# SyncE's order at the end of an image: the edge row moved ahead of the four corner transfers of the ring

## Chip, cores and metric

The program runs on one core of one Trainium2 chip. The metric is the device time of one launch in microseconds (us); less is better. The times are those of whole launches, and one execution was also profiled.

## The reference, cut to what matters

```python
def step(u, _):
    ux, uy, uxx, uxy, uyy = _derivs(u)                  # 3x3 Sobel stencils, and stencils of stencils
    g2 = ux * ux + uy * uy
    ...                                                 # curvatures K and H from the five fields
    diff = jnp.clip(alpha * K + beta * H, -1.0, 1.0)
    u = u + DT * diff
    u = jnp.pad(u[:, :, 1:-1, 1:-1], ((0, 0), (0, 0), (1, 1), (1, 1)), mode='edge')
    return (u, None)
u, _ = jax.lax.scan(step, x, None, length=10)
x = 0.7 * u + 0.3 * x                                   # the "blend"
out = conv(relu(conv(x, w1) + b1), w2) + b2 + x         # second stage
```

There are 8 x 16 = 128 images of 512 x 512 in float32. After each of the ten steps the outermost pixels of an image are overwritten with their inner neighbours: first the edge columns, then the edge rows (which read corners that the columns have set).

## The kernel before, in words

**Tiling.** An image is cut into patches so that 128 partitions hold 2048 pixels each; partition p holds every 16th row and every 8th column. An image has two halves ("chunks") of 1024 pixels a partition. Four images are in work at once, so one step is eight chunks, c = 0 to 7, and each image is carried through ten steps. There are 32 rounds of four images. Neighbouring pixels lie in other partitions, so a step needs matmuls over partitions (the stencils, L654) and a "ring" of neighbours shifted by a row or a column, which is copied inside SBUF by DMA.

**The ring.** `exchange(image, j, part)` (L288) issues four DMAs from `tame_split` to `tame_halo`. Part 0 holds left, right, top and bottom (520, 520, 260 and 260 KB); part 1 holds the four corners (65 KB each, from and to 4 partitions). The stencils of both chunks of an image wait for all eight.

**Periods.** All engines walk through periods k = 0 to 7 of a step. In period k TensorE works on chunk k, VectorE ends chunks k-1 and k-2, and SyncE sets the edges of chunk k-2: `edge_columns` (two small DMAs, L297, after `updated`), and `edge_rows` (one DMA, L305 for even and L307 for odd chunks, after both columns have landed). In every even period SyncE also issues the ring of the image that comes two periods later. GpSimd issues one DMA a period, which adds K to U (`add_k`, L379).

**End of an image.** In the tenth step (body "closing", and the first two periods of the next one, "opening") each chunk is also blended into the staging tile: VectorE's `blend` (`tame_stage<-tame_U,tame_stage`, listed under L532) in the period after its edges. It waits for the chunk's edge row (`rows_done`) and for ScalarE's `scale` of the staged input (L468). It stands on VectorE ahead of `curvature_k`, which TensorE's `uxx` waits for. After a blend, SyncE loads the next image's half (`load_half`, L277, 512 KB), after the second half of an image it stores the staging tile (`store`, L311, 1 MB), and in periods 5 and 7 of closing it loads a staging tile (`load_stage`, L283, 1 MB) once the store before has landed. All of these are in SyncE's one order, and each of its instructions waits for the one ahead.

In the first-stage body a chunk "ends" when its tenth step is done: chunks 0 to 5 in periods 2 to 7 of closing, chunks 6 and 7 in periods 0 and 1 of opening. Only in the even ones of these periods is there a part 1 of a ring to issue beside an edge row: chunks 0, 2, 4 and 6.

Of the kernel before, what the change touches and what calls it, by code (L numbers as in the profile page):

```python
# [54 lines left out]
def place(c):  # L55

    return c // 2 + (1 - c % 2) * (PC // 2)
# [50 lines left out]
def curvature_flow(nc, keep, semaphores, x, alpha, beta, stencils, mixed, tame):  # L108
# [21 lines left out]
    with ExitStack() as ctx:  # L130
# [80 lines left out]
        def half(c):  # L211
            return U[:, c % CHUNKS // 2, c % 2 * HALF:(c % 2 + 1) * HALF]

        def half_rows(c):
            return half(c).rearrange("p (y x) -> p y x", x=PX)
# [12 lines left out]
        def done(t, c):  # L228
            return t + 2 * (c + 1)

        def split_done(t, c):
            return t + 2 * (c + 1) + BODY

        def exists(kind, c):
            return not (kind == "first" and c < 0) and not (kind == "tail" and c >= 0)

        def ends(kind, c):
            return (kind in ("closing", "last") and c >= 0) or (kind in ("opening", "tail") and c < 0)

        def goes_on(kind, c):  # L240

            return not (kind == "last" and c >= 0) and not (kind == "tail" and c < 0)
# [7 lines left out]
        def walk(eng, period):  # L250
            def body(t, kind, r=None):
                for k in range(CHUNKS):
                    period(t, k, kind, r)

            body(0, "first")
            with eng.Fori(BODY, (STEPS - 1) * BODY, BODY) as t:
                body(t, "middle")
            with eng.Fori(0, ROUNDS - 1) as r:
                body(r * (STEPS * BODY) + (STEPS - 1) * BODY, "closing", r)
                body(r * (STEPS * BODY) + STEPS * BODY, "opening", r)  # L260
                with eng.Fori((STEPS + 1) * BODY, (2 * STEPS - 1) * BODY, BODY) as t:
                    body(r * (STEPS * BODY) + t, "middle")
            body((ROUNDS * STEPS - 1) * BODY, "last", ROUNDS - 1)
            body(ROUNDS * STEPS * BODY, "tail", ROUNDS - 1)
# [3 lines left out]
        @block.sync  # L268
        def _(sp):
            sp.dma_start(a_raw, alpha.partition_broadcast(P)).then_inc(params_in, 16)  # L270
            sp.dma_start(b_raw, beta.partition_broadcast(P)).then_inc(params_in, 16)
            sp.dma_start(stage[0][:, 0:MATRICES * P].rearrange("p (n m) -> p n m", m=P),
                         stencils[:, 0:MATRICES, :]).then_inc(stencils_in, 16)
            sp.dma_start(unit[:, :, :], stencils[:, MATRICES:, :]).then_inc(unit_in, 16)

            def load_half(r, k):
                sp.dma_start(half(k), x[bass.ds(r * SLOTS + k // 2, 1), :, k % 2 * HALF:(k % 2 + 1) * HALF].rearrange(  # L277
                    "o p c -> (o p) c")).then_inc(x_in[k], 16)

            def load_stage(r, i):  # L280
                sp.wait_ge(stored[i % 2], r * 32 + (i // 2 * 16 + 16))
                sp.sem_inc(stage_free, 1)
                sp.dma_start(stage[i % 2][:, :], x[bass.ds(r * SLOTS + i, 1), :, :].rearrange(  # L283
                    "o p c -> (o p) c")).then_inc(stage_in[i % 2], 16)

            def exchange(i, j, part):
                for first, step, n, shift, to, apart in RING[part * 4:part * 4 + 4]:
                    sp.dma_start(halo[j][to:to + (n - 1) * apart + 1:apart, :, :].bitcast(F32),  # L288
                                 split[i][first:first + (n - 1) * step + 1:step, :,
                                          BEFORE + shift:BEFORE + shift + RUN].bitcast(F32)).then_inc(halo_in[i], 16)  # L290

            def edge_columns(t, c):
                u = half_rows(c)
                sp.wait_ge(updated, done(t, c))
                signal = columns_done[c % CHUNKS]
                for edge, inner, px in ((0, 1, 0), (PC - 1, PC - 2, PX - 1)):
                    sp.dma_start(u[place(edge):P:PC, :, px:px + 1], u[place(inner):P:PC, :, px:px + 1],  # L297
                                 allow_slow_non_contiguous=True).then_inc(signal, 16)

            def edge_rows(t, c):  # L300
                u = half_rows(c)
                sp.wait_ge(columns_done[c % CHUNKS], t * 2 + (32 if c >= 0 else 0))
                signal = rows_done[c % CHUNKS]
                if c % 2 == 0:
                    sp.dma_start(u[0:PC, 0:1, :], u[PC:2 * PC, 0:1, :]).then_inc(signal, 16)  # L305
                else:
                    sp.dma_start(u[P - PC:P, ROWS - 1:ROWS, :], u[P - 2 * PC:P - PC, ROWS - 1:ROWS, :]).then_inc(signal, 16)  # L307

            def store(r, i):
                image = mixed[bass.ds(r // (C // SLOTS), 1), :, bass.ds(r % (C // SLOTS) * SLOTS + i, 1), :, :]  # L310
                sp.dma_start(image.rearrange("b r o g c -> (b r o) g c"), stage[i % 2][:, :]).then_inc(stored[i % 2], 16)  # L311

            def period(t, k, kind, r):
                filling = k % 2 == 0 and kind != "tail" and not (kind == "last" and k == CHUNKS - 2)
                image, j = (k + 2) % CHUNKS // 2, (k + 2) % 4 // 2
                if filling:
                    sp.wait_ge(lo_ready, split_done(t, k - 5))
                    sp.sem_inc(split_whole, 1)
                    if not (kind == "first" and k == 0):
                        sp.wait_ge(product[LAST_FIELD], done(t, k - 1))  # L320
                    exchange(image, j, 0)
                c = k - 3
                ending = exists(kind, c) and ends(kind, c)
                if ending:
                    sp.wait_ge(blended, r * CHUNKS + (c % CHUNKS + 1))
                    sp.sem_inc(stage_done, 1)
                    if goes_on(kind, c):
                        load_half(r + 1, c % CHUNKS)
                c = k - 2
                if exists(kind, c):  # L330
                    edge_columns(t, c)
                if filling:
                    exchange(image, j, 1)
                if exists(kind, c):
                    edge_rows(t, c)
                c = k - 3
                if ending and c % 2:
                    store(r, c % CHUNKS // 2)
                if k in (5, 7) and kind in ("closing", "last"):
                    load_stage(r, k // 2)  # L340
                if k in (6, 7) and kind in ("first", "opening"):
                    load_stage(0 if kind == "first" else r + 1, k - 6)

            for k in range(CHUNKS):
                load_half(0, k)
            for j in range(2):
                sp.sem_inc(stored[j], 16)
            sp.wait_ge(stencils_rounded, 1)
            sp.wait_ge(ring_zeroed, 1)
            sp.wait_ge(lo_ready, 4)  # L350
            exchange(0, 0, 0)
            exchange(0, 0, 1)
            walk(sp, period)
            for j in range(2):
                sp.wait_ge(stored[j], ROUNDS * 32 + 16)
# [675 lines left out]
```

## Time and profile before

| what | us |
|---|---|
| median of 3 runs | 36501.38 |
| lowest and highest of them | 36483.21, 36510.54 |
| profiled execution, its time | 36543.25 |
| its span | 36541.3 |
| TensorE busy in the span | 33388.0 |
| VectorE busy | 31917.9 |
| ScalarE busy | 32731.5 |

The profiled execution took 41.9 us more than the median of the runs, and its span is 2.0 us under its own time. A steady round of 8 chunks runs from about 1.3 ms to 32.8 ms of the span; the second stage fills the rest and has none of the code in question.

### The profile page before, as it was taken

The page shows a single profiled execution, that of the slowest core. Times are in us where ns is not written, and L with a number is a line of the kernel's source. Part 1 is how long each engine was busy: PE and PEld are TensorE (multiplying, and loading weights), DVE is VectorE, ACT ScalarE, POOL GpSimd, SP SyncE. Part 2 cuts the span into 40 slices and gives each one's busy share as a digit, 9 for nine tenths or more (in the row PEclk, how much of TensorE's full clock was granted, in tenths as well). Part 3 has the DMA queues.
Part 4 walks back from the last instruction along what each step waited for, and adds up shares of the span by engine and source line. Part 5 has one row for each costly group of instructions (what it writes and reads, how often), then busy time and mean ns, then how long its engine had stood idle before and what let it go on. Part 6 is the DMA issues. An engine that isn't in the chain of part 4 may idle for free. (4 is left out here: it accounts for less than half of the span.)

```text
span 36541.3 us, 454649 instructions
## 1 busy us (share of the span) xinstructions
PE 33388.0 (91%) x126400; PEld 23480.4 (64%) x126400; DVE 31917.9 (87%) x30550; ACT 32731.5 (90%) x33722; POOL 21233.1 (58%) x10245
## 2 busy tenths in 40 slices
PE   5999999999999999999999999999999999989999
PEld 3666666666666666666666666666666666666666
DVE  8999999999999999999999999999999999991111
ACT  5999999999999999999999999999999999993333
POOL 3666666666666666666666666666666666660000
PEclk9999999999999999999999999999999999999999
DMA  6555555555555555555555555555555555553333
GB/s 222 129 129 130 128 124 122 130 128 129 129 129 129 129 129 124 124 129 129 129 129 129 129 129 129 125 121 129 129 130 129 129 129 129 129 115 86 87 87 87
DMA packets 3056143, 4603.99 MB, mean 126 GB/s; under 512 B 2307140, under 2 KB 2307268, under 8 KB 2733380
## 3 DMA queue, kind: packets, MB, share of 16 engines
q1 hardware_dynamic: 2686276, 3247.70, 35.7%
q0 software_dynamic: 368640, 1342.34, 19.7%
q8 instruction: 475, 7.78, 0.1%
q14 instruction: 752, 6.16, 0.1%
HBM read 582.33 MB, written 268.44 MB: 23 GB/s over the span
## 5 line engine op out<-in xcount | busy, mean ns | idle before, releaser
L654 PE MATMUL tame_slot<-tame_split,tame_M 128*128 128x512 f32 x51200 | 14727.2, 410 | 2992.1 <-ACT tame_ux L415 1768.1
L654 PEld LDWEIGHTS tame_slot<-tame_split,tame_M 128*128 128x128 f32 x51200 | 9360.1, 190 | 7792.7 <-ACT tame_ux L415 3880.2
L654 PE MATMUL tame_slot<-tame_halo,tame_M 128*128 128x512 f32 x51200 | 14283.6, 401 | 25.3 <-issue 25.0
L654 PEld LDWEIGHTS tame_slot<-tame_halo,tame_M 128*128 128x128 f32 x51200 | 9735.2, 190 | 2518.6 <-issue 31.4
L367 POOL TENSOR_TENSOR tame_ux<-tame_ux,tame_uy 128x1024 f32<-128x1024 f32 x2560 | 6146.6, 2401 | 2765.6 <-DVE tame_uy L532 2765.5
L379 POOL DMA_DIRECT2D tame_U<-tame_slope x2560 | 2241.6, 876 | 8448.8 <-DVE tame_slope L586 8181.0
L373 POOL TENSOR_TENSOR tame_ux<-tame_ux,tame_cross 128x1024 f32<-128x1024 f32 x2560 | 6939.1, 2711 | 0.0
L361 POOL TENSOR_TENSOR tame_split<-tame_U,tame_split 128x1024 fp32r<-128x1024 f32 x2560 | 6710.6, 2622 | 21.6 <-ACT tame_split L404 21.6
L442 ACT ACTIVATE tame_slope<-tame_slope 128x2048 f32<-128x2048 f32 x2560 | 4912.2, 1919 | 234.9
L664 PE MATMUL tame_slot<-tame_uxy,tame_unit 128*128 128x512 f32 x10240 | 4815.1, 593 | 6.3 <-DVE tame_slot L555 4.2
L532 DVE SCALAR_TENSOR_TENSOR tame_cross<-tame_cross,tame_slot 128x1024 f32<-128x1024 f32 x2560 | 3122.3, 1220 | 664.2 <-issue 613.3
L532 DVE SCALAR_TENSOR_TENSOR tame_U<-tame_slope,tame_par,tame_U 128x1024 f32<-128x1024 f32 x2560 | 3307.5, 1292 | 14.4 <-DMA tame_U<-tame_slope 14.0
L532 DVE SCALAR_TENSOR_TENSOR tame_slope<-tame_slot,tame_par,tame_slope 128x1024 f32<-128x1024 f32 x2560 | 3258.3, 1273 | 4.1 <-PE tame_slot L664 3.2
L555 DVE TENSOR_TENSOR tame_slot<-tame_uyy,tame_slot 128x1024 f32<-128x1024 f32 x2560 | 3128.5, 1222 | 0.0
L551 DVE TENSOR_TENSOR tame_cross<-tame_cross,tame_slot 128x1024 f32<-128x1024 f32 x2560 | 3092.5, 1208 | 40.1 <-PE tame_slot L654 39.8
L580 DVE TENSOR_TENSOR tame_slope<-tame_ux,tame_slot 128x1024 f32<-128x1024 f32 x2560 | 3108.3, 1214 | 3.9 <-issue 3.9
L532 DVE SCALAR_TENSOR_TENSOR tame_uy<-tame_uy,tame_slot 128x1024 f32<-128x1024 f32 x2560 | 3107.9, 1214 | 0.0
L532 DVE SCALAR_TENSOR_TENSOR tame_slope<-tame_ux,tame_uy 128x1024 f32<-128x1024 f32 x2560 | 3105.2, 1213 | 2.8 <-ACT tame_uy L421 2.7
L532 DVE SCALAR_TENSOR_TENSOR tame_ux<-tame_ux,tame_slot 128x1024 f32<-128x1024 f32 x2560 | 3094.1, 1209 | 8.6 <-ACT tame_uyy L427 8.2
L437 ACT ACTIVATE tame_slope<-tame_slope 128x1024 f32<-128x1024 f32 x2560 | 2755.6, 1076 | 280.9 <-DVE tame_slope L532 274.3
L870 DVE SCALAR_TENSOR_TENSOR res<-po,vec,xin 96x512 f32<-96x512 f32 x672 | 501.6, 746 | 2839.3 <-PE po L891 2839.3
L823 ACT ACTIVATE hid<-ph,vec 128x512 f32<-128x512 f32 x2064 | 754.6, 437 | 2421.8 <-PE ph L891 2421.8
(75 smaller groups left out, 40812.1 us busy)
## 6 DMA issues: line engine op xcount, KB each, us to landing
tame_halo<-tame_split SPq DMA_DIRECT2D x2560, 520.0 KB
tame_U<-tame_slope POOLq DMA_DIRECT2D x2560, 512.0 KB, 5.2
tame_halo<-tame_split SPq DMA_DIRECT2D x2560, 260.0 KB
tame_halo<-tame_split SPq DMA_DIRECT2D x5120, 65.0 KB
tame_U<-in_x SPq DMA_DIRECT2D x256, 512.0 KB, 6.0
tame_stage<-in_x SPq DMA_DIRECT2D x128, 1024.0 KB, 6.1
mixed<-tame_stage SPq DMA_DIRECT2D x128, 1024.0 KB, 6.5
out<-res SPq DMA_DIRECT2D x672, 192.0 KB
```

What stands on the lines that cost most here:

```text
L361: nc.gpsimd.tensor_tensor(split_rows(c, 1), half_rows(c), split_rows(c, 0).bitcast(F32), ALU.subtract).then_inc(lo_ready, 2)
L367: nc.gpsimd.tensor_tensor(ux2[c % 2][:, :], ux2[c % 2][:, :], uy2[c % 2][:, :], ALU.add).then_inc(sum_h, 2)
L373: nc.gpsimd.tensor_tensor(ux2[c % 2][:, :], ux2[c % 2][:, :], cross[c % 2][:, :], ALU.add).then_inc(num_h_ready, 2)
L379: pool.dma_start(half(c), slope[c % 2][:, 1, :], accum_op=ALU.add).then_inc(k_added[c % 2], 16)
L437: nc.scalar.activation(slope[c % 2][:, 1, :], slope[c % 2][:, 0, :], ACT.Square).then_inc(slope2_ready, 2)
L442: nc.scalar.activation(both, both, ACT.Ln, bias=EPS).then_inc(logs_ready, 2)
L532: return nc.vector.scalar_tensor_tensor(out=out, in0=a, scalar=s, in1=b, op0=op0, op1=op1)
L551: nc.vector.tensor_tensor(cross[c % 2][:, :], cross[c % 2][:, :], ps["uy"][:, :], ALU.mult).then_inc(cross_ready, 2)
L555: nc.vector.tensor_tensor(ps["uxx"][:, :], uyy[:, :], ps["uxx"][:, :], ALU.mult).then_inc(prod_k, 2)
L580: nc.vector.tensor_tensor(slope[c % 2][:, 0, :], ux2[c % 2][:, :], inverse[:, :], ALU.mult).then_inc(h_ready, 2)
L654: last = nc.tensor.matmul(ps[name][:, b * BANK:(b + 1) * BANK], M[0:lanes, matrix, :], rows(c, part)[:, b * y:(b + 1) * y, :], start=(n < ...
L664: last = nc.tensor.matmul(ps["uxx"][:, b * BANK:(b + 1) * BANK], unit[:, 0, :], uxy2[:, b * BANK:(b + 1) * BANK], start=False, stop=True, ...
```

## The change

For a chunk whose image ends, `edge_rows` is called directly behind `edge_columns`, and part 1 of the ring behind it. For every other chunk the order stays as it was. Nothing is added or removed: one DMA and its wait are moved ahead of four DMAs.

```diff
                 c = k - 2
+                late = exists(kind, c) and not ends(kind, c)
                 if exists(kind, c):
                     edge_columns(t, c)
+                    if not late:
+                        edge_rows(t, c)
                 if filling:
                     exchange(image, j, 1)
-                if exists(kind, c):
+                if late:
                     edge_rows(t, c)
                 c = k - 3
                 if ending and c % 2:
```

SyncE in period 6 of closing: `tame_U<-tame_U 16x16x1` are the edge columns of chunk 4, `8x64` its edge row, `4x2x2080 x4` the four corners, and `mixed<-tame_stage` the store of the image before:

```order
 L297 DMA tame_U<-tame_U 16x16x1 [waits updated]
 L297 DMA tame_U<-tame_U 16x16x1
+L305 DMA tame_U<-tame_U 8x64 [waits columns_done4]
 L288 DMA tame_halo<-tame_split 4x2x2080 x4
-L305 DMA tame_U<-tame_U 8x64 [waits columns_done4]
 L311 ISA
 L311 DMA mixed<-tame_stage 16x8x2048
```

The edge row and its wait for the columns now stand ahead of the corners, and the corners stand directly ahead of the store.

SyncE in period 0 of opening, the same for chunk 6:

```order
 L297 DMA tame_U<-tame_U 16x16x1 [waits updated]
 L297 DMA tame_U<-tame_U 16x16x1
+L302 REGISTER_ALU
+L305 DMA tame_U<-tame_U 8x64 [waits columns_done6]
 L288 DMA tame_halo<-tame_split 4x2x2080 x4
-L302 REGISTER_ALU
-L305 DMA tame_U<-tame_U 8x64 [waits columns_done6]
 L311 ISA
 L311 DMA mixed<-tame_stage 16x8x2048
```

Here too the four corners move behind the wait. Chunks 0 and 2 are moved alike in periods 2 and 4 of closing.

What stands on SyncE between these two places (period 7 of closing, and the start of opening), in the kernel before; it is the same after the change:

```order
L277 DMA tame_U<-in_x 128x1024
L297 DMA tame_U<-tame_U 16x16x1 [waits updated]
L297 DMA tame_U<-tame_U 16x16x1
L307 DMA tame_U<-tame_U 8x64 [waits columns_done5]
L283 ISA [waits stored1]
L283 DMA tame_stage<-in_x 128x2048
L317 REGISTER_ALU
L288 DMA tame_halo<-tame_split 32x2x2080 [waits lo_ready,uxx_product]
```

Nothing moves here, but all of it waits for what was issued ahead of it: chunk 5's row waits for chunk 5's columns, the staging load stands behind that row, and part 0 of the next ring behind the load.

## Rows read from the trace of the kernel before

**Rows 1.** The page's span and its busy times of the engines.
```profile
span 36541.3 us, 454649 instructions
...
PE 33388.0 (91%) x126400; PEld 23480.4 (64%) x126400; DVE 31917.9 (87%) x30550; ACT 32731.5 (90%) x33722; POOL 21233.1 (58%) x10245
```

**Rows 2.** Waits of the whole span (us, times, longest), then who waited for L305.
```profile
DVE tame_stage L532 <- DMA tame_U<-tame_U: 282.0, 63, 6.1
...
  DVE tame_stage L532: 277.8, 62
```

**Rows 3.** Timeline of SyncE's queue, first round: start, us until issued, line, DMA.
```profile
1360.40 3.75 SPq L288 DMA_DIRECT2D tame_halo<-tame_split  x4
...
1389.12 5.16 SPq L297 DMA_DIRECT2D tame_U<-tame_U  x2
1394.33 2.58 SPq L288 DMA_DIRECT2D tame_halo<-tame_split  x4
1399.04 0.70 SPq L305 DMA_DIRECT2D tame_U<-tame_U  x1
1400.03 0.65 SPq L311 DMA_DIRECT2D mixed<-tame_stage  x1
1402.37 0.35 SPq L277 DMA_DIRECT2D tame_U<-in_x  x1
1404.52 1.26 SPq L297 DMA_DIRECT2D tame_U<-tame_U  x2
1410.68 0.71 SPq L307 DMA_DIRECT2D tame_U<-tame_U  x1
1411.68 0.34 SPq L283 DMA_DIRECT2D tame_stage<-in_x  x1
1414.97 3.94 SPq L288 DMA_DIRECT2D tame_halo<-tame_split  x4
1420.86 4.32 SPq L297 DMA_DIRECT2D tame_U<-tame_U  x2
...
1429.63 0.71 SPq L305 DMA_DIRECT2D tame_U<-tame_U  x1
```

**Rows 4.** Timeline of VectorE, the blends of chunks 3 to 6 in that round.
```profile
1383.14 1.32 DVE L532 SCALAR_TENSOR_TENSOR tame_stage<-tame_U,tame_stage 128x1024 f32<-128x1024 f32 x1 [0.69 <-ACT tame_stage L468]
...
1400.88 1.23 DVE L532 SCALAR_TENSOR_TENSOR tame_stage<-tame_U,tame_stage 128x1024 f32<-128x1024 f32 x1 [4.57 <-DMA tame_U<-tame_U]
...
1416.28 1.23 DVE L532 SCALAR_TENSOR_TENSOR tame_stage<-tame_U,tame_stage 128x1024 f32<-128x1024 f32 x1 [1.50 <-ACT tame_stage L468]
...
1432.14 1.23 DVE L532 SCALAR_TENSOR_TENSOR tame_stage<-tame_U,tame_stage 128x1024 f32<-128x1024 f32 x1 [2.77 <-DMA tame_U<-tame_U]
```

**Rows 5.** Timeline, the last of the 62 pairs of edge row and waiting blend.
```profile
31838.29 0.71 SPq L305 DMA_DIRECT2D tame_U<-tame_U  x1
...
31841.15 1.23 DVE L532 SCALAR_TENSOR_TENSOR tame_stage<-tame_U,tame_stage 128x1024 f32<-128x1024 f32 x1 [5.31 <-DMA tame_U<-tame_U]
```

**Rows 6.** Issue to landing: columns of chunk 4, then the staging load at 1411.68.
```profile
DMA to landing us min/median/max: 6.4/7.1/7.8
...
DMA to landing us min/median/max: 4.9/4.9/4.9
```

**Rows 7.** Stretches of that round: us, busy times, granted clock, DMA share, GB/s.
```profile
1398.00:1400.50 2.50, 1.86 (x8) 1.37 (x8) 0.00 (x0) 2.50 (x3) 0.00 (x0) 1.00 0.10 37
1401.00:1410.50 9.50, 5.58 (x16) 3.95 (x16) 9.50 (x9) 4.47 (x4) 3.91 (x3) 0.70 0.93 221
1410.50:1412.50 2.00, 2.00 (x8) 1.57 (x7) 1.89 (x3) 1.03 (x2) 2.00 (x2) 0.73 0.01 1
1412.50:1416.00 3.50, 3.29 (x11) 1.70 (x11) 1.54 (x2) 3.50 (x4) 2.37 (x1) 1.00 0.81 300
1416.00:1426.00 10.00, 8.62 (x36) 6.29 (x35) 9.72 (x9) 9.60 (x10) 4.03 (x3) 1.00 0.98 236
1426.00:1429.50 3.50, 3.15 (x11) 1.60 (x10) 3.26 (x4) 3.50 (x5) 3.50 (x2) 1.00 0.65 129
```

**Rows 8.** Timeline of TensorE: the first stencil of the next round's chunk 0.
```profile
1407.63 2.04 PE L654 MATMUL tame_slot<-tame_split,tame_M 128*128 128x512 f32 x4 [1.58 <-DVE tame_ux L532]
```

## Prediction

> **What bounds the kernel now.** I read the page first. TensorE is busy for 91% of the span, ScalarE for 90% and VectorE for 87% [rows 1], so in the steady steps all three are near their limit and SyncE only has to be in time. The change touches SyncE alone, and only at the end of images, so I went from the page to the waits. There the blend stands with 282.0 us in 63 waits for an edge DMA, and the look from the other side says that 62 of these are for L305, the edge row of an even chunk, with 277.8 us [rows 2]. That is two in each of 31 rounds (the last round has no ring to fill), 4.5 us each.
>
> Which two, the timelines tell. Blends of undisturbed chunks wait 0.69 us for ScalarE; chunk 4 waits 4.57 us and chunk 6 waits 2.77 us for the row DMA, and chunk 5 between them 1.50 us for ScalarE [rows 4]. From chunk 3's blend to chunk 4's it is 17.74 us. The longer wait is passed on in full, since VectorE has work without a gap in the rest of that period, and TensorE and ScalarE hang on it. Chunks 0 and 2, which the change moves too, have no such wait. So what the change is worth hangs on the two places with chunk 4 and chunk 6, 31 times each, and one us there is 31 us in the total.
>
> **Why the row is late there.** In SyncE's queue [rows 3] the columns of chunk 4 need 5.16 us to be issued, the corners go out from 1394.33 to 1396.91, and then SyncE stands still until 1399.04, when it issues the row. The columns took 6.4 to 7.8 us from issue to landing [rows 6]: the second, issued about 1392.6, landed about 1399.0. So SyncE waited 2.13 us for the columns with the corners already out. The corners in front cost the row no issue time: after the change its wait ends at the same moment, if the columns land at the same moment. At chunk 6 it is alike: the row goes out at 1429.63, well behind the corners.
>
> **What moves, part by part.**
>
> Issue of the row: nothing gained at chunks 4 and 6, by the above. At chunks 0 and 2 it goes out earlier (for chunk 2 it stood behind 3.75 us of corners [rows 3]), where the blend does not wait for it; worth nothing.
>
> Landing of the row: in the first round the blend of chunk 4 started 1.84 us behind the issue of its row (1400.88 - 1399.04), that of chunk 6 2.51 us behind (1432.14 - 1429.63) [rows 3, 4], the last pair 2.86 us [rows 5]. Over the 62 pairs, of which these are the first and the last, the mean is 2.38 us, and the shortest is about 1.8 us. I read the excess as the tail of the corners, which are still moving on some engines when the row comes. With the corners behind the row I take 1.84 us for all: 0.54 x 62 = **33 us gained**. Bounds: nothing, if the excess is other traffic; and if the corners slow the columns too, up to 1.3 us a place, 81 us, since the time from the columns' issue to the blend is 11.8 us at chunk 4 (1389.12 to 1400.88) and 11.3 us at chunk 6, and with the row's excess gone and the columns in time it could be about 10.3.
>
> The Trainium skill (DMA: Bandwidth & Descriptors, Queues, rings and completion order) says that a copy is split over up to 16 rings, always the lowest-numbered, and that each ring is consumed in its order. By that rule a row of 8 partitions shares its rings with corners of 4 partitions and waits behind them, while columns that were issued ahead of the corners don't. The spread from 1.84 to 2.86 us agrees with it. By the rule the gain would be the 33 us and not the 81.
>
> Issue of the corners: they no longer go out at 1394.33 but behind the row, at 1399.04 + 0.71 = 1399.8. Four took 2.58 us here and 3.75 us in a calmer place [rows 3]; I take 3.2, so SyncE is free at 1403.0 where it was free at 1399.8. **Everything behind on SyncE is 3.2 us late** (2.6 to 3.8): the store of 1 MB, issued at 1403.3 for 1400.03; load_half about 1404.2 for 1402.37; the columns of chunk 5 hardly, since they wait for `updated` until 1404.52.
>
> The Trainium skill (the same page, Anatomy of one DMA) has a rule that speaks against this order: DMA engines never wait for a semaphore, the issuing sequencer does, so what stands behind a wait isn't even queued. Here the row's wait falls in a stretch where the DMA engines have a share of 0.10 [rows 7], and the corners would have filled it.
>
> What this does to the DMA engines: after 1401 they were busy without a pause, share 0.93, until 1410.5 with the store, the load, the columns of chunk 5 and GpSimd's add [rows 7], and the columns of chunk 5 landed at the end of it, since L307 went out at 1410.68 [rows 3]. The block starts 3.2 us later, so it ends about 1413.9 and chunk 5's row goes out there. With 1.84 us it is there at 1415.7; the blend of chunk 5 starts at 1416.28, held by ScalarE [rows 4]. That cover of 0.6 us just hides it: cost 0, and up to 1 us (31 us in all) where it is thinner.
>
> But behind chunk 5's row on SyncE stands the staging load (1 MB, 1411.68, 4.9 us to landing [rows 3, 6]). It fell into an idle stretch (share 0.01 until 1412.5), and its data was through at 1416, just where part 0 of the next ring, issued at 1414.97, began to move [rows 3, 7]. Issued at 1414.9 instead, its data comes in front of the ring's: the ring, the load of chunk 5's successor and then chunk 6's columns are pushed back. From 1416 to 1426 the engines have a share of 0.98 and then 0.65 [rows 7], so a push at the front comes out nearly whole at chunk 6's columns, and the blend of chunk 6 waits for just those. At full size this is 3.2 us; the tail at 0.65 and rounds in which chunk 5's columns come earlier than here give a part back. I take 2.5 us: 2.5 x 31 = **78 us lost** (bounds 0, if the engines take the load in their gaps, and 3.8 x 31 = 118).
>
> Behind chunk 6 the same shift of 3.2 us meets chunk 7, but no staging load stands there and the next ring starts after a pause; I take 0 there, at most 1 us x 31.
>
> The corners themselves: issued until 1403.0, their stencils start at 1407.63 [rows 8], where TensorE waits for VectorE. Landed within 4.6 us of issue they cost nothing; in that stretch they have only the store beside them. I take 0.
>
> **Sum.** -33 + 78 = +45 us. Against the profiled execution of 36543.3 that is 36588; its 41.9 us above the median of the runs is no part of this, so for the median I predict 36501.4 + 45 = **36546 us**.
>
> **The rivals.**
>
> 1. Gain alone. The late staging load slips in beside the ring's parts, since single stretches of the ring may be slow for reasons other than busy engines. For it: 33 us of gain need nothing further. Against it: the share of 0.98. Time: 36501 - 33 = 36468 (to 36440).
> 2. Columns and row both come earlier, as the corners are out of the engines' way: 1.3 us x 62 = 81 us with no push, 36420. For it: chunk 4's columns need 4.7 us after the end of their issue. Against: they are ahead of the corners in the queue.
> 3. TensorE waits for the corners at the start of the next round's chunks 0 and 2, or the push is whole and chunks 5 and 7 wait as well. Place: the first stencil at 1407.63. It decides if the corners need more than 4.6 us after their issue; every us beyond is 62 us. With 1 us there and the sum above 36608; with 118 + 31 + 31 - 33 instead, 36648. For it: corners have been slow to land beside other traffic. Against: the engines are nearly empty when they now go out.
> 4. No effect at all: the row's excess is other traffic and the push is hidden, 36501.
>
> A longer or shorter wait also meets TensorE's clock: in the stretch behind chunk 4's wait the granted clock averages 0.70, part of it at the lower level (1.2 of 2.4 GHz) after TensorE stood still [rows 7], and the matmuls at 1407.63 are slow [rows 8]. Such a drop follows both waits already in most rounds, so I count no more than 10 us for it, either way.
>
> **How the numbers follow.** My sum with its neighbours, +10 to +90 us: 0.43. Rival 1: 0.25. Rival 4: 0.07. Rival 2: 0.10. Rival 3: 0.15. About 0.2% of the time, 73 us, is what a measurement of this kernel can tell from no change. Over +73 lie rival 3 and a quarter of my own case: 0.26. Under -73 lies most of rival 2: 0.10. The rest, 0.64, is within. The range takes in rival 1 whole, half of rival 2 and the near part of rival 3: 36430 to 36610. The likeliest case has 36511 to 36591 for itself.
>
> **What would show it.** In the changed trace the row of chunk 4 should go out in 1.84 us before its blend, with the corners behind it; chunk 4's wait should be about 0.5 us shorter than its mean of before. L307 of chunk 5 should stand about 13 us behind chunk 4's blend where it stood 9.8, the staging load behind it, and the wait of chunk 6's blend should be about 2 us longer. If chunk 6's wait is no longer than before, the push is wrong and rival 1 holds; if TensorE has a new wait for a `tame_halo` DMA, rival 3 does. The wait of the blends for DMAs, 282.0 us before, should come to about 330 us. I am wrong if the columns themselves land earlier, or if the four corners go out in far less than 2.6 us.

## The result and the profile after

The changed kernel takes 36584.1 us (median of 19 runs, 36558.8 to 36604.8) where the kernel before takes 36502.7 us (19 runs, 36472.0 to 36523.8). The ratio is 1.0021, with a 95% interval of 1.0015 to 1.0028: slower by 81 us, small but clear. Forecast were +45 us (36546 us) and a range from 36430 to 36610 us.

The blend's waits, in the view of waits of the changed kernel (us, times, longest), then the blend's waits for L305 and for L307 by themselves:

```profile
DVE tame_stage L535 <- DMA tame_U<-tame_U: 419.5, 120, 7.8
...
DVE tame_stage L535 <- ACT tame_stage L471: 106.2, 134, 1.7
...
  DVE tame_stage L535: 286.5, 62
...
  DVE tame_stage L535: 133.0, 58
```

Against [rows 2] the waits for an even chunk's row (L305) are as many as before and a little longer, 286.5 us for 277.8. What is new are 58 waits, 133.0 us, for L307, the row of an odd chunk, a line that the change doesn't touch. The blend's waits for ScalarE went down by 60.4 us (166.6 us in 191 times before), as they are now covered by the longer ones. Sum: 137.5 - 60.4 = 77 us more, close to the launch's 81 us. (The two profiled executions themselves are 61.5 us apart, see below the table.)

SyncE's queue in the first round of the changed kernel, timeline, as in [rows 3]:

```profile
1386.07 5.61 SPq L297 DMA_DIRECT2D tame_U<-tame_U  x2
1396.23 0.72 SPq L305 DMA_DIRECT2D tame_U<-tame_U  x1
1397.01 2.35 SPq L288 DMA_DIRECT2D tame_halo<-tame_split  x4
1399.64 0.66 SPq L311 DMA_DIRECT2D mixed<-tame_stage  x1
1400.66 0.35 SPq L277 DMA_DIRECT2D tame_U<-in_x  x1
1401.73 3.76 SPq L297 DMA_DIRECT2D tame_U<-tame_U  x2
1411.81 0.74 SPq L307 DMA_DIRECT2D tame_U<-tame_U  x1
1412.84 0.34 SPq L283 DMA_DIRECT2D tame_stage<-in_x  x1
1413.37 4.68 SPq L288 DMA_DIRECT2D tame_halo<-tame_split  x4
```

And VectorE's blends of chunks 4 to 7, as in [rows 4]:

```profile
1398.09 1.23 DVE L535 SCALAR_TENSOR_TENSOR tame_stage<-tame_U,tame_stage 128x1024 f32<-128x1024 f32 x1 [4.86 <-DMA tame_U<-tame_U]
1413.71 1.23 DVE L535 SCALAR_TENSOR_TENSOR tame_stage<-tame_U,tame_stage 128x1024 f32<-128x1024 f32 x1 [2.54 <-DMA tame_U<-tame_U]
1433.15 1.23 DVE L535 SCALAR_TENSOR_TENSOR tame_stage<-tame_U,tame_stage 128x1024 f32<-128x1024 f32 x1 [6.35 <-DMA tame_U<-tame_U]
1448.60 1.22 DVE L535 SCALAR_TENSOR_TENSOR tame_stage<-tame_U,tame_stage 128x1024 f32<-128x1024 f32 x1 [2.37 <-DMA tame_U<-tame_U]
```

What to see: the row of chunk 4 is followed by its blend after 1.86 us, with the corners behind it, as the change means it. But the store stands 1.55 us behind that blend, where it stood 0.85 us ahead of it [rows 3, 4], and the row of chunk 5 goes out 13.7 us behind the blend of chunk 4, where it was 9.8. Chunk 5's blend, held by ScalarE before, now waits 2.54 us for that row, and chunk 7's waits 2.37 us for its own.

The DMA engines in that round (us, busy times, granted clock, DMA share, GB/s), as in [rows 7]:

```profile
1395.00:1397.50 2.50, 1.86 (x8) 1.43 (x8) 0.00 (x0) 2.50 (x4) 0.00 (x0) 1.00 0.02 3
1398.00:1411.00 13.00, 9.95 (x28) 6.85 (x28) 12.81 (x12) 7.48 (x8) 7.21 (x4) 0.74 0.77 182
1411.00:1413.00 2.00, 1.64 (x7) 1.01 (x6) 0.17 (x1) 2.00 (x3) 1.09 (x1) 1.00 0.04 8
...
1416.50:1428.00 11.50, 9.44 (x36) 6.33 (x35) 10.19 (x10) 10.14 (x10) 8.31 (x4) 1.00 0.97 236
```

While SyncE waits for the columns the engines have nothing (0.02), then a block of 13 us at 0.77 where there was one of 9.5 us at 0.93: the same store, load, columns and add, started later, with the corners in it too.

From blend to blend, the mean over 31 rounds, worked out from the starts of the blends in both traces:

| from chunk to chunk | before, us | after, us | x 31, us |
|---|---|---|---|
| 3 to 4 | 17.87 | 17.49 | -12 |
| 4 to 5 | 14.57 | 15.76 | +37 |
| 5 to 6 | 17.36 | 18.24 | +27 |
| 6 to 7 | 14.56 | 15.43 | +27 |

The sum is +79 us. The stretches up to chunk 3 are the same to 0.02 us. The rest of a round, from chunk 7's blend through the other nine steps to the next chunk 0, took 907.91 us before and 907.42 after; it lies between 907.1 and 909.0 us in all thirteen traces, so these 0.5 us are not put down to the change. They are why the two profiled executions differ by only 61.5 us. A single stretch is not exact either: experiment 1 leaves the order at chunks 4 to 7 as it was and has 14.28 and 17.68 us from chunk 4 to 5 and from 5 to 6, for 14.57 and 17.36. So a row of the table can be off by some 10 us; the sum of those two is the same to 0.03 us.

GpSimd's add beside chunk 5's columns, before and then in the changed kernel, timeline of the first round:

```profile
1405.81 0.87 POOL L379 DMA_DIRECT2D tame_U<-tame_slope  x1 [8.55 <-DVE tame_slope L586]
```

```profile
1403.01 0.88 POOL L382 DMA_DIRECT2D tame_U<-tame_slope  x1 [8.85 <-DVE tame_slope L589]
```

Before, both columns were issued by 1405.78 [rows 3], just ahead of the add. In the changed kernel their issue takes 3.76 us, until 1405.49, and the second is still being issued when the add is out (1403.89). Before, the second column landed ahead of the add in all 31 rounds at chunk 5 and in 27 of 31 at chunk 7; after the change in none. Then both land together, 13.4 to 13.7 us behind the blend before, instead of 9.1 and 7.9 us for the column.

### The profile page after: what moved, and what is told of

The parts are those of the page before. It is cut to its first block and busy times, and to the rows that moved or that the text cites. A ratio compares the mean times of both kernels' runs of the same rounds, so it can differ in the third digit from the quotient of the medians.

```text
span 36602.9 us, 454649 instructions
## 1 busy us (share of the span) xinstructions
PE 33401.0 (91%) x126400; PEld 23460.5 (64%) x126400; DVE 31879.6 (87%) x30550; ACT 32759.2 (89%) x33722; POOL 21255.2 (58%) x10245
```

## The experiments

All were timed beside the kernel before on the same chip, so each ratio has its own "before" (36475 to 36503 us). The changed kernel stands at 1.0021 throughout. Mean waits by chunk, here and in the expectations, are over all 32 rounds; the last round waits 0.7, 0, 0 and 4.3 us at chunks 4 to 7 in nearly every run (in experiment 2, 7.4 at chunk 7). Times from blend to blend and from row to blend are means over the other 31.

**1. Only the calm places.** The change at chunks 0 and 2, not at 4 and 6 (the edit is to the changed kernel):

```diff
-                late = exists(kind, c) and not ends(kind, c)
+                late = exists(kind, c) and not (ends(kind, c) and 0 <= c < 4)
```

> The row goes ahead of the corners only at chunks 0 and 2 of an ending image; chunks 4 and 6 keep the order of before. Theory: all of the change's cost and gain lies at chunks 4 to 7, where blends wait for transfers, so this is the kernel before, 36503 us within 15 us. Rival (the two calm places cost or give something too, by the later store and load behind them): at least a quarter of the change's +81 us, or a gain of more than 20 us.

Measured: 1.0001 (0.9992 to 1.0010), 36483.1 us. Chunks 0 and 2 are worth nothing that can be told, and the effect comes from the two places where blends wait.

**2. Only the late store.** The kernel before, rows and corners in their old order, the two stores behind the next blend:

```diff
                     sp.sem_inc(stage_done, 1)
+                    if c % CHUNKS in (4, 6):
+                        store(r, c % CHUNKS // 2 - 1)
...
-                if ending and c % 2:
+                if ending and c % CHUNKS in (1, 7):
                     store(r, c % CHUNKS // 2)
```

> The kernel before, rows and corners where they were; only the stores that the change makes late (images of chunks 3 and 5) go out behind the next blend, at about 1.3 us behind the blends of chunks 4 and 6, where the changed kernel has them at 1.5 us and the kernel before at 1.4 us ahead. Theory (the later store and load ahead of the columns of chunks 5 and 7 make the loss): L307 of chunks 5 and 7 moves from 9.1 and 7.9 us to 12.5 to 14 us behind the blend before it, both blends get a wait for their row of 2.0 to 2.4 us, and the launch is 60 to 120 us over the kernel before. Rival (the corners' own data, now in that block, or SyncE's time for them is needed): L307 moves by less than 2 us and the launch by less than 40 us.

Measured: 1.0032 (1.0020 to 1.0044), 36605.7 us. SyncE's queue and the blends of its first round, timeline:

```profile
1394.97 0.66 SPq L311 DMA_DIRECT2D mixed<-tame_stage  x1
1395.82 0.43 SPq L277 DMA_DIRECT2D tame_U<-in_x  x1
1397.04 3.73 SPq L297 DMA_DIRECT2D tame_U<-tame_U  x2
1407.03 0.71 SPq L307 DMA_DIRECT2D tame_U<-tame_U  x1
```

```profile
1393.40 1.22 DVE L534 SCALAR_TENSOR_TENSOR tame_stage<-tame_U,tame_stage 128x1024 f32<-128x1024 f32 x1 [4.48 <-DMA tame_U<-tame_U]
1408.92 1.23 DVE L534 SCALAR_TENSOR_TENSOR tame_stage<-tame_U,tame_stage 128x1024 f32<-128x1024 f32 x1 [1.59 <-DMA tame_U<-tame_U]
```

The store stands 1.57 us behind chunk 4's blend, and chunk 5's row 13.6 us behind it: the changed kernel's numbers, with no corner and no row moved. Over the rounds chunks 5 and 7 wait 2.29 and 2.32 us (2.26 and 2.15 in the changed kernel, 1.05 and 1.23 before), and chunk 6's wait is 5.34 us. So the late store alone makes the loss: 1.0032, about 117 us. That it is more than the changed kernel's loss the times don't settle, as the intervals overlap. The stretches from blend to blend do: they sum to +112 us here and to +79 us there, and of the 33 us between, 14 lie in the stretch to chunk 4 and 17 in that to chunk 6, where the changed kernel's row lands faster.

**3. The store back in its place.** The changed kernel with the order row, store, corners (the store's lines further down are gone):

```diff
+                if ending and (k - 3) % 2:
+                    store(r, (k - 3) % CHUNKS // 2)
                 if filling:
                     exchange(image, j, 1)
```

> As the change, but the store of 1 MB goes out between row and corners, where the kernel before has it; only the corners are late. Theory: the loss comes from the store and the load that went out about 3 us later and reach into the columns of chunks 5 and 7. With the store back in time the block in front of those columns starts as before, the new waits of the blends of chunks 5 and 7 (2.26 and 2.15 us on average, 1.05 and 1.23 before) go back by at least half, and the launch takes 36500 to 36545 us. Rival (the corners themselves, now moved into that block, hold the columns up, wherever the store stands): the waits of chunks 5 and 7 stay at about 2.2 us and the time at 36570 to 36600. Corners could also come too late for TensorE's first stencil: then a wait for tame_halo appears and the time goes over 36600.

Measured: 1.0053 (1.0039 to 1.0067), 36671.8 us. Neither theory, but the warning at its end. The view of waits, and TensorE's first stencil of the next round's chunk 0 in the timeline:

```profile
PE tame_slot L656 <- DMA tame_halo<-tame_split: 737.0, 63, 415.0
PEld tame_slot L656 <- DMA tame_halo<-tame_split: 355.0, 66, 6.4
```

```profile
1410.73 1.65 PE L656 MATMUL tame_slot<-tame_split,tame_M 128*128 128x512 f32 x3 [5.01 <-DMA tame_halo<-tame_split]
```

One wait of 415 us at the start of the program is in every version; the 62 others, 5.2 us each, are new. Behind the store the four corners needed 5.78 us to be issued instead of 2.35, and came too late. On the store this run says less than it was made for, as TensorE's stall moves the blends of chunks 5 and 7 too; their rows go out 13.7 us behind the blend before, store early or not, as the columns now stand behind the slow corners. It shows how near the changed kernel is to that edge.

**4. The staging load behind the ring.** The changed kernel, with the load of period 7 behind part 0 of the next ring:

```diff
                     exchange(image, j, 0)
+                if k == 0 and kind in ("opening", "tail"):
+                    load_stage(r, 3)
...
-                if k in (5, 7) and kind in ("closing", "last"):
+                if k == 5 and kind in ("closing", "last"):
```

> As the change, but the staging load of period 7 goes out behind the first half of the next ring instead of ahead of it. Theory of the prediction (the late staging load pushes ring, load and columns of chunk 6): the wait of chunk 6's blend (4.77 us on average) falls by 1 to 2.5 us and the launch to 36510 to 36555 us. Rival (the wait of chunk 6 grew because later traffic in general is denser, and the same megabyte behind the ring is as much in the way of chunk 6's columns): that wait stays within 0.4 us and the time within 15 us of 36584.

Measured: 1.0034 (1.0022 to 1.0046), 36603.6 us; chunk 6's wait went up from 4.77 to 6.57 us. Both expectations missed. The megabyte is in front of the load and the columns in either place. From chunk 5's blend to chunk 6's it is 20.13 us for 18.24: the columns start to be issued 6.86 us behind chunk 5's blend instead of 5.19, and the row follows 11.4 us later for 11.2. So what the move cost is the later issue of the columns. My reading, not tried by itself, is that ahead of the ring a part of the megabyte still runs in an idle stretch and behind it none does. ScalarE also waits for this load now, 30.5 us in 23 waits.

**5. One store out of the way.** The changed kernel with the store of chunk 5's image behind chunk 7's row:

```diff
-                if ending and c % 2:
+                if ending and c % 2 and c % CHUNKS != 5:
                     store(r, c % CHUNKS // 2)
+                if ending and c % CHUNKS == 6:
+                    store(r, 2)
```

> The changed kernel, with one store (the image of chunk 5) taken out of the block ahead of chunk 7's columns and put behind chunk 7's row. Theory: the columns of chunk 7 land at least 3 us earlier, the wait of chunk 7's blend falls from 2.15 to about 1.2 us, the others stay, and the launch is 25 to 45 us under the changed kernel, at 1.0010 to 1.0015 of the kernel before. Rival (corners and load are enough to hold chunk 7's columns up): the wait stays over 1.8 us and the ratio at 1.002.

Measured: 1.0015 (1.0006 to 1.0024), 36532.1 us. Timeline of its queue and the blend of chunk 7:

```profile
1433.92 1.25 SPq L297 DMA_DIRECT2D tame_U<-tame_U  x2
1437.06 0.74 SPq L307 DMA_DIRECT2D tame_U<-tame_U  x1
```

```profile
1445.59 1.23 DVE L537 SCALAR_TENSOR_TENSOR tame_stage<-tame_U,tame_stage 128x1024 f32<-128x1024 f32 x1 [1.63 <-ACT tame_stage L473]
```

Over the rounds the columns of chunk 7 are through 1.9 us behind the end of their issue (6.2 in the changed kernel), and in all 31 ahead of GpSimd's add, the blend waits for ScalarE again, and its mean wait is 1.12 us. The corners and the load, still ahead of those columns, don't hold them up. The intervals of 1.0015 and 1.0021 overlap; the wait is what tells.

**6. Corners ahead of the columns.** The kernel before, and where an image ends: corners, columns, row.

```diff
+                early = filling and exists(kind, c) and ends(kind, c)
+                if early:
+                    exchange(image, j, 1)
                 if exists(kind, c):
                     edge_columns(t, c)
-                if filling:
+                if filling and not early:
                     exchange(image, j, 1)
```

> The kernel before with the other way to free the row: where an image ends, the corners go out ahead of the columns, and the row directly behind the columns. Theory (rows land in 1.8 us where no corner is behind the columns; the columns land only when ring, load and GpSimd's add are through, and the corners are a small part of that): row to blend falls from 2.4 to about 1.9 us, the store stays early, no new wait at chunks 5 and 7: 10 to 50 us under the kernel before. Rival (corners ahead of the columns hold these up by their full time of 1.5 to 3 us): chunk 4 and 6 wait longer and the launch is 30 to 150 us over it.

Measured: 1.0034 (1.0022 to 1.0046), 36611.1 us; the rival was right. Its queue, timeline:

```profile
1380.87 1.80 SPq L277 DMA_DIRECT2D tame_U<-in_x  x1
1382.71 6.91 SPq L288 DMA_DIRECT2D tame_halo<-tame_split  x4
1389.75 1.33 SPq L297 DMA_DIRECT2D tame_U<-tame_U  x2
1394.79 0.73 SPq L305 DMA_DIRECT2D tame_U<-tame_U  x1
```

Rows land fast (row to blend 1.88 us over the rounds), but behind ring and load SyncE needs 6.91 us to issue four corners. The columns of chunk 4 go out 13.0 us behind chunk 3's blend instead of 6.0, its row 18.0 instead of 15.5, and chunks 4 and 6 wait 6.5 and 6.3 us.

**7. The load behind the row.** The kernel before, and in all periods with a ring `load_half` behind the edge row instead of ahead of the columns:

```diff
-                    if goes_on(kind, c):
+                    if goes_on(kind, c) and not filling:
                         load_half(r + 1, c % CHUNKS)
...
                 c = k - 3
+                if ending and goes_on(kind, c) and filling:
+                    load_half(r + 1, c % CHUNKS)
```

> The kernel before with one other edit: in periods with a ring, load_half of an ending image goes out behind the edge row instead of ahead of the columns. Theory: what holds the rows of chunks 4 and 6 is the traffic in front of their columns (ring and 512 KB of load), not the corners; without the load in front the columns land 1.5 to 3 us earlier, and each of the two blend waits (4.6 and 4.1 us) falls by as much: 36503 less 60 to 180 us, 36320 to 36440. Rival (the columns are held by the ring and by GpSimd's add alone): no more than 30 us gained. Another (ScalarE's next high part waits for the load, which now lands 4 to 5 us later): a new wait of ScalarE for the load, and a time over 36503.

Measured: 0.9992 (0.9983 to 1.0001), 36443.5 us beside 36475.4: less than the theory's 60 us, and by time just short of clear. The two waits fell to 3.64 and 2.72 us, but chunk 2's row, calm before, became late (blend to blend 14.21 us for 13.72). The rows of chunks 4 and 6 go out about 2 us earlier (13.3 and 13.1 us behind the blend before, for 15.5 and 15.0), but with the corners still ahead of them they take longer to land: from row to blend 3.58 and 2.88 us instead of 2.39 and 2.36. ScalarE has a new wait:

```profile
ACT tame_split L406 <- DMA tame_U<-in_x: 100.4, 77, 2.8
```

**8. Both of these.** Corners ahead of the columns and the load behind the row (the edits of 6 and 7 together).

> Both: corners ahead of the columns, and in periods with a ring load_half behind the row. Theory: the columns have only ring, corners and add ahead, the row nothing; the waits of chunks 4 and 6 (3.64 and 2.72 us with the load behind the row alone) fall by another 1 us each, to about 2.6 and 1.8: 36475 less 60 to 120 us. Rival (ScalarE's high part waits for the late load in each of those periods, 1.3 us before, and takes the gain): no faster than with the load behind the row alone, ratio 0.9992.

Measured: 1.0018 (1.0009 to 1.0027), 36538.4 us; the rival was right on the side and it came out worse than it said. Rows land in 1.88 us, with the load right behind them, but the waits of chunks 4 and 6 are back at 4.58 and 4.78 us, since the columns go out 11.4 and 11.8 us behind the blend before instead of 3.9. ScalarE's wait for the load is 262.9 us.

**9. The change where it can't hurt.** Row first at chunk 6 alone, and the store of chunk 5's image behind chunk 7's row (an edit to the changed kernel; the store's lines are those of experiment 5):

```diff
-                late = exists(kind, c) and not ends(kind, c)
+                late = exists(kind, c) and not (ends(kind, c) and c % CHUNKS == 6)
```

> The change at chunk 6 alone (row ahead of the corners), chunks 0, 2 and 4 in the order of before, and the store of chunk 5's image behind chunk 7's row. Theory: this keeps the gain (row to blend of chunk 6 from 2.4 to 1.9 us) and leaves nothing late ahead of chunk 7's columns; chunk 5 has no late store and there is no late staging load. Blend waits of chunks 5 and 7 stay at 0.9 to 1.3 us, that of chunk 6 falls by about 0.5 us: 5 to 30 us under the kernel before, ratio 0.9992 to 1.0000. Rival (the row's landing behind the corners was never the limit, or the late corners cost TensorE): no gain, or over 1.0005.

Measured: 0.9995 (0.9986 to 1.0004), 36485.8 us. Row to blend at chunk 6 is 1.88 us, the waits of chunks 5 and 7 are 1.03 and 1.12 us, and chunk 6's is 3.53 us. As expected by size, and by size not to be told from no change.

**10. The edits of 9 and 7 together.**

> The same together with load_half behind the edge row in periods with a ring (0.9992 on its own). Theory: the two add up, since with the load gone from ahead of the columns the row of chunk 6 lands 2.8 us behind its issue, and without the corners 1.8: chunk 6's wait falls from 2.7 to about 1.7 us, ratio 0.9978 to 0.9990. Rival (the load is now behind the corners too and ScalarE waits for it longer than the row gains): ratio 0.9992 or more.

Measured: 0.9996 (0.9987 to 1.0005), 36484.2 us. Chunk 6's wait fell to 1.87 us, but the load now stands behind the corners too, ScalarE's wait for it grew to 192.2 us, and from chunk 6's blend to chunk 7's it is 15.83 us instead of 14.2. The rival was right.

**11. The load behind the row at chunks 4 and 6 only.** Only the two periods with a late row:

```diff
-                    if goes_on(kind, c):
+                    if goes_on(kind, c) and c % CHUNKS not in (3, 5):
                         load_half(r + 1, c % CHUNKS)
...
+                if ending and goes_on(kind, c) and c % CHUNKS in (3, 5):
+                    load_half(r + 1, c % CHUNKS)
```

> The kernel before with load_half behind the edge row only in the two periods where the blend waits for that row (chunks 4 and 6); chunks 2 and 0 keep their order. With it in all periods with a ring, the waits of chunks 4 and 6 fell to 3.64 and 2.72 us, but chunk 2's blend got a longer one (14.21 instead of 13.72 us from blend to blend). Theory: without that, 31 times 0.5 us more are saved: ratio 0.9984 to 0.9992, 20 to 60 us under the kernel before. Rival (the waits of chunks 4 and 6 fell because of what was moved at chunk 2, or ScalarE's waits for the late load take it all): 0.9995 or more.

Measured: 0.9976 (0.9967 to 0.9985), 36419.1 us beside 36503.1: faster than both kernels, by more than expected. Its waits, and its queue at chunk 4:

```profile
DVE tame_stage L534 <- DMA tame_U<-tame_U: 206.4, 64, 4.4
...
ACT tame_split L406 <- DMA tame_U<-in_x: 69.9, 55, 3.2
```

```profile
1380.40 4.47 SPq L297 DMA_DIRECT2D tame_U<-tame_U  x2
1384.92 3.91 SPq L288 DMA_DIRECT2D tame_halo<-tame_split  x4
1389.73 0.70 SPq L305 DMA_DIRECT2D tame_U<-tame_U  x1
1390.64 0.35 SPq L277 DMA_DIRECT2D tame_U<-in_x  x1
1391.26 0.65 SPq L311 DMA_DIRECT2D mixed<-tame_stage  x1
```

The row goes out 9.3 us behind the start of the columns' issue (9.9 before, [rows 3]), and the columns' issue starts earlier as the load's is gone from ahead of it. Blend to blend it is 16.88 and 15.91 us at chunks 4 and 6, 17.87 and 17.36 before: 2.4 us in a round, 76 us in all, and chunks 5 and 7 are 0.3 us shorter each. Against experiment 7 it is less clear than the ratios look: their intervals touch (0.9985 and 0.9983), and in the two traces the stretches up to chunk 7 differ by 0.46 us a round, 14 us in all, most of it at chunks 2 and 3.

## Why the prediction came out as it did

The side was right and the time is in the range. The terms that the prediction worked out were of the right kind, but most of the loss came from two that it had put at 0. With the measured gain and push alone the sum would be +11 us; that it came out near is in part luck, as the push was taken 35 us too large and the two zeros 64 us too small.

- **Where it counts.** The two places with chunks 4 and 6, 31 times each: right. Without them it is worth nothing that can be told (experiment 1).
- **The landing of the row, -33 us.** Right. Row to blend is 1.87 us over the 62 pairs instead of 2.38, so 0.51 x 62 = 32 us; none took more than 1.89 us, where it was up to 3.6 before. The columns themselves didn't come faster: issue to landing 6.4 to 7.6 us at chunk 4 in the first round for 6.4 to 7.8 [rows 6]. Rival 2 is out. Experiments 2 (order of before, 2.32 us) and 9 (row first at chunk 6, 1.88 us) agree.
- **SyncE free 3.2 us later.** Right: the store stands 2.9 us later against the blend of chunk 4 (1.5 us behind it for 1.4 ahead of it, over the rounds). The corners took 2.35 us to issue, not 3.2.
- **Chunk 5's row at about 13 us.** Near, but for a shift that is wrong: L307 goes out 13.7 us behind chunk 4's blend over the rounds. It stood at 9.1, so it moved by 4.6 us and not by 3.2. The prediction passed the store's lateness on as it was.
- **Cover of chunk 5's blend, cost 0.** This step failed: 37 us. I held the late row (there at 1415.7, 14.8 us behind chunk 4's blend) against a blend at 1416.28, 15.4 us behind it, and called the 0.6 us a cover. The row comes at 15.6 us, 0.8 later than taken, and the blend of before stands at 14.57 us on average, 0.8 earlier: it was one of the latest of the 31 (13.8 to 15.4), half of the difference being its ScalarE wait of 1.50 us for 1.09 on average. Together that is the 1 us that is missing. The price I named for a thinner cover, up to 1 us in each round, is about what came (1.2 us).
- **Chunk 7, cost 0.** This step failed: 27 us. Shifted by 3.2 us its row would have kept a cover of 1.6 us on average, but it went out 13.5 us behind chunk 6's blend for 7.9, which is 5.6 us later. I looked at what stands behind chunk 7's row (no staging load) and not at the row itself. Experiment 5 shows that the late store is what does it, experiment 2 that it does so without the corners. Why 2.9 us of lateness become 4.6 and 5.6 is a reading of the traces and was not tried by itself: the second column used to land ahead of GpSimd's add, and now lands with it.
- **The push on chunk 6, +78 us.** Right in kind and too large: chunk 6 takes 0.88 us more with 0.5 us of row gain inside, so the push is 1.4 us and not 2.5, 43 us. Experiment 2, where chunk 6's row has no gain, has 18.80 us from chunk 5 to 6 for 17.36, again 1.4. Why the full 2.5 us don't arrive stays open; my reading is that part of the megabyte still runs ahead of the ring. No run moves the staging load alone against the kernel before.
- **Corners in time for TensorE.** Right: TensorE's one wait for `tame_halo` is that at the program's start, as before. Rival 3's first half did not come, but is close (experiment 3); of its second half, that chunks 5 and 7 wait came, and that the push is whole did not.
- **The clock, at most 10 us.** In the 12 us behind the blends of chunks 5 and 7 the granted clock averages 0.94 in the changed kernel and 1.00 before, as TensorE now stands still there too; behind chunks 4 and 6 it is 0.85 for 0.81 and 0.84. The blends of chunks 5 to 7 are released by their rows in 88 of 93 cases, so I see no price of it there; it was not measured by itself.
- **The waits for DMAs, 330 us.** They came to 419.5, as the waits of chunks 5 and 7 were not in the forecast.

Summed again: -32 + 37 + 27 + 43 = +75 us, measured +81.

## What to carry to other kernels

A transfer moved behind a wait makes everything behind it in that queue late, and the bill comes to whoever stands there, here a store whose lateness hit the next two chunks. The lateness isn't passed on one for one: 2.9 us at the store were 4.6 and 5.6 us at the next two rows. And the distance to the next waiter is taken as a mean over the rounds, with its spread, as one round can show a cover that most don't have. When a small transfer is late, ask what is queued ahead of it before asking what is beside it: the corners next to the row were worth 0.5 us, the load ahead of the columns 1 to 1.4. And an edit that helps where a wait stands can make a new one where none does (chunk 2's in experiment 7, 0.5 us), so it is put only where the wait is.

## What the runs showed of the hardware

- Issuing is not a fixed cost. The same four corner DMAs took SyncE 2.35 us with the DMA engines idle, 5.78 us right behind a 1 MB store, and 6.91 us behind ring and load.
- What is issued right behind the row didn't slow it: 1.87 us from issue to blend with the corners behind, 1.88 us with the load of 512 KB behind (experiment 8). With the corners ahead it took 2.38 us on average and up to 3.6, and 3.58 us on average at chunk 4 in experiment 7, where the load is gone from ahead of the columns.
- Where a load stands in the queue shows in its reader's waits: ScalarE doesn't wait for the halves in the kernel before; it waited 69.9 us in all with the load right behind the row at two places, 100.4 us at all four, and 192.2 us with the corners between at chunk 6.
- Two small transfers (the columns, 1 KB each) land 1.8 to 2.3 us behind their issue at chunks 1 to 3, and need 7.3 to 8.8 us behind store, load and add (chunks 5 and 7 of the changed kernel), from issue to landing.
